# A Newton iteration's squares crossed in all six steps, and one quarter of their copy moved from ScalarE to VectorE

## What is computed

```
K = kernel_2                                  # softmax, 64x64 per image and head
V = 1 / max(sum(K, axis=-2)) * K^T
for _ in range(6):
    KV = K @ V
    V = 0.25 * V @ (13 I - KV @ (15 I - KV @ (7 I - KV)))
```

## Time and profile before

| | |
|---|---|
| median of 3 runs | 690.59 us (689.09 to 691.2) |
| profiled execution, its own time | 694.64 us |
| span in the profile | 692.8 us |
| TensorE matmul busy | 656.4 us (95%) |
| TensorE weight load busy | 574.3 us (83%) |
| VectorE busy | 496.1 us (72%) |
| ScalarE busy | 385.5 us (56%) |
| granted TensorE clock, mean | 0.988 of full |

### The profile page before, as it was taken

How to read it: one execution, slowest core, us unless ns; L and a number is a source line. 1 busy time by engine, 2 the same in 40 slices (tenths; PEclk the granted TensorE clock), 3 DMA queues, 4 the chain that set the end, 5 groups by cost and what they waited for, 6 DMA issues and landing times.

```text
span 692.8 us, 29942 instructions
## 1 busy us (share of the span) xinstructions
PE 656.4 (95%) x13218; PEld 574.3 (83%) x13218; DVE 496.1 (72%) x1351; ACT 385.5 (56%) x1045; POOL 106.5 (15%) x328
## 2 busy tenths in 40 slices
PE   4878999999999999999999998899999999999998
PEld 2667888888888888888888787688999999999997
DVE  5566878888888888888888986576557547556644
ACT  0245776766776776676676766744444444444442
POOL 1212123223212312312312400110000000000000
PEclk9988999999999999999999999999999999999999
DMA  8792121111111111111100000000000000000000
GB/s 310 260 286 82 35 65 34 35 64 35 36 63 35 50 48 35 52 47 35 34 4 5 4 4 4 4 1 2 0 24 1 1 0 24 2 1 23 1 1 23
DMA packets 13425, 30.64 MB, mean 44 GB/s; under 512 B 1264, under 2 KB 7536, under 8 KB 13040
## 3 DMA queue, kind: packets, MB, share of 16 engines
q1 hardware_dynamic: 13296, 28.73, 12.7%
HBM read 27.16 MB, written 1.57 MB: 41 GB/s over the span
## 4 chain that ended last, share of the span: by engine, by line
PE 87%; DVE 6%; ACT 3%; issue 2%; DMA 1%; SPq 1%; POOL 0%; DVEq 0%; POOLq 0%
PE ps L409 29%; PE ps L574 18%; PE ps L564 16%; PE ps L296 6%; PE ps L313 2%; PE ps L374 2%; PE ps L427 2%; PE ps L356 2%; PE ps L314 1%; PE ps L348 1%; DVE uu L857 1%; DVE se L813 1%; DVE sst L811 1%; PE ps L440 1%; PE ps L328 1%
## 5 line engine op out<-in xcount | busy, mean ns | idle before, releaser
L919 DVE SCALAR_TENSOR_TENSOR acc<-ps,comb,acc 128x192 f32<-128x192 f32 x256 | 89.1, 411 | 84.0 <-PE ps L574 83.9
L574 PE MATMUL ps<-w_sb,work 128*128 128x192 f32 x768 | 140.3, 326 | 0.7 <-ACT work L744 0.7
L574 PEld LDWEIGHTS ps<-w_sb,work 128*128 128x128 f32 x768 | 129.3, 189 | 9.0 <-issue 1.1
L744 ACT ACTIVATE work<-ps 128x512 f32<-128x512 f32 x96 | 57.3, 597 | 138.7 <-PE ps L564 138.7
L409 PEld LDWEIGHTS ps<-rr 64*64 64x64 f32 x3840 | 98.2, 135 | 20.3 <-issue 11.9
L409 PE MATMUL ps<-rr 64*64 64x64 f32 x3840 | 110.8, 223 | 4.0 <-issue 3.2
L409 PE MATMUL ps<-uu,qq 64*64 64x64 f32 x4608 | 99.4, 226 | 11.9 <-DVE uu L857 10.3
L857 DVE SCALAR_TENSOR_TENSOR uu<-rr,qq 128x384 f32<-128x384 f32 x160 | 86.5, 563 | 32.5 <-ACT qq L651 24.2
L409 PEld LDWEIGHTS ps<-uu,qq 64*64 64x64 f32 x4608 | 82.9, 135 | 29.5 <-DVE uu L857 19.1
L658 ACT ACTIVATE rr<-ps 128x384 f32<-128x384 f32 x160 | 73.8, 489 | 57.7 <-PE ps L409 57.3
L296 PE MATMUL ps<-weff,xtb 128*128 128x193 f32 x240 | 51.3, 351 | 1.1 <-DVE t L768 1.1
(11 more groups left out here) (142 smaller groups left out, 1070.0 us busy)
## 6 DMA issues: line engine op xcount, KB each, us to landing
xtb<-xt_dram SPq DMA_DIRECT2D x16, 512.0 KB, 3.8
work<-x_dram SPq DMA_DIRECT2D x16, 512.0 KB, 4.1
wsh<-ws_dram SPq DMA_DIRECT2D x10, 288.0 KB, 5.7
w_sb<-w_dram SPq DMA_DIRECT2D x1, 2304.0 KB, 22.3
w_a<-w_dram SPq DMA_DIRECT2D x1, 1536.0 KB, 10.5
w_b<-w_dram SPq DMA_DIRECT2D x2, 768.0 KB, 14.7
out_dram<-acc SPq DMA_DIRECT2D x3, 384.0 KB, 2.6
mult<-copies_dram SPq DMA_DIRECT2D x1, 512.0 KB, 8.2
```

Of the source, the lines that this page charges most:

```text
L574: last = pe.matmul(ps[:, 2 + 2 * (e % 2) + j // 2, (j % 2) * DIM:(j % 2 + 1) * DIM], hid[:, n % 4, j * P:(j + 1) * P], w2_sb[:, c, :], sta ...
L744: act.activation(hid[:, n % 4, :], ps[:, UPB[n % 3], :], ACT.Gelu_apprx_tanh).then_inc(gelu_done, 1)
L919: last = dve.scalar_tensor_tensor(out=a, in0=ps[:, 2 + 2 * (e % 2) + j // 2, (j % 2) * DIM:(j % 2 + 1) * DIM], scalar=comb[:, g * GT + j, ...
```

## The change

`CROSSED` becomes all six steps, and a new table `HALVED` with all six steps is added. In a step of `HALVED`, ScalarE copies image 0 of lane 0 and that half of image 1 which goes to partitions 0 to 63; VectorE copies the half that goes from PSUM partitions 0 to 63 to partitions 64 to 127 of qq. VectorE does this at the head of newton_sum, on the same semaphore (square_done) that ScalarE waits for, and then waits for its own copy (q_half) before uu. ScalarE's second copy raises q_ready by 2, so that the counts stay as they were.

```
-CROSSED = (1, 2, 3, 5)
+CROSSED = (0, 1, 2, 3, 4, 5)
+HALVED = (0, 1, 2, 3, 4, 5)
...
                     q = qq[:, lane].rearrange("p i h n -> p i (h n)")
-                    if lane == 0 and k in CROSSED:
+                    if lane == 0 and k in HALVED:
+                        act.activation(q[:, 0], ps[:, 0, 0:LC], ACT.Copy).then_inc(q_ready, 1)
+                        act.activation(q[0:64, 1], ps[64:128, 1, 0:LC], ACT.Copy).then_inc(q_ready, 2)
+                    elif lane == 0 and k in CROSSED:
                         act.activation(q[:, 0], ps[:, 0, 0:LC], ACT.Copy).then_inc(q_ready, 1)
                         for a in (0, 64):
                             act.activation(q[a:a + 64, 1], ps[64 - a:128 - a, 1, 0:LC], ACT.Copy).then_inc(q_ready, 1)
...
             def newton_sum(k, t, lane):
                 n = 12 * t + 2 * k + lane
                 src = r0 if k == 0 else rr
+                if lane == 0 and k in HALVED:
+                    dve.wait_ge(square_done, n + 1)
+                    dve.tensor_copy(qq[64:128, 0, 1].rearrange("p h n -> p (h n)"), ps[0:64, 1, 0:LC]).then_inc(q_half, 1)
+                    dve.wait_ge(q_half, len(HALVED) * t + HALVED.index(k) + 1)
                 dve.wait_ge(q_ready, 4 * (STEPS * t + k) + 3 + lane)
                 dve.scalar_tensor_tensor(out=uu[:, lane], in0=src[:, lane], scalar=3.0, in1=qq[:, lane],
                                          op0=ALU.mult, op1=ALU.add).then_inc(u_ready, 1)
```

More of the change, by code:

```diff
@@ L159, in vit_block_kernel @@
         y_copied, square_done = sems("y_copied square_done")
-        q_ready, u_ready, prod_done, r_ready, o_done = sems("q_ready u_ready prod_done r_ready o_done")
+        q_half, q_ready, u_ready, prod_done, r_ready, o_done = sems("q_half q_ready u_ready prod_done r_ready o_done")
         o_copied, proj_done, h2_ready = sems("o_copied proj_done h2_ready")
```

## The result

The changed kernel takes **703.97 us** (702.89 to 705.29, four runs) against 690.89 for the kernel before on the same chip: a ratio of 1.0193, 95% interval 1.0175 to 1.021. It is 13.1 us slower, clear of noise. The forecast was 698.0, and the range ended at 702. The sign was right and the size was not.

A forecast was written before the change was run, and what follows sets the result against it. TensorE was taken to bound the kernel (87% of the chain), with VectorE nearly full. Regular tiles 5.4, stopped tiles 0.3, tiles 13 and 14 3.0, tile 15 -1.1, tile 0 -0.2: +7.4 on 690.59 gives 698.0 us; range 691 to 702.

The forecast's parts named there:

- The copy: VectorE's new PSUM copy ahead of lane 0's uu: 0.355 us, costing 0.50 us where VectorE is late.
- Step 1: Newton step 1, where VectorE comes late: uu of both lanes and the products come later, +0.50 us a tile.
- Steps 0, 2 and 5: Newton steps where the copy makes uu or the products slightly later: +0.10, +0.03 and +0.05 us a tile.
- Step 3: Newton step 3, where VectorE idles 0.83 us for ScalarE: lane 0's uu 0.35 us earlier, the step -0.39 us.
- Step 4: Newton step 4, VectorE late again: lane 0's uu late by 0.47 us, 0.25 of it slack; step +0.31 us.
- The sum: All six Newton steps of a regular tile together: +0.60 us a tile, 5.4 us over nine regular tiles.
- tiles 13 and 14: Tiles without token matmuls on TensorE, so steps 2 and 3 also hang on VectorE: +3.0 us together.
- The last tile: Tile 15, where VectorE is idle and the change helps: -1.1 us.
- Step 1 of tiles 3, 8 and 9: TensorE stops 0.6 to 0.7 us inside these squares, covering the copy's price; 0.1 us left each.
- the overlap of the copy with its predecessor: Rival: the copy overlaps its predecessor, costing 0.39 us where VectorE is late; +0.24 a tile, 692.5 us; chance 0.14.
- The saving: Rival: cheap copy, so TensorE's 0.35 and ScalarE's 0.33 us come through; 676 at the ceiling, halfway 685; chance 0.17.
- The copy is longer than its row: Rival: VectorE slowed by 0.13 us at each late place beside others' work; +4.5 on top, 702.5 us; chance 0.12.

The follow-up runs named there:

- the changed kernel with the late add: The changed kernel with GpSimd's residual add moved behind its low_tokens; 702.93 us, ratio 1.0149 to the kernel before.

## Why the prediction was right in sign and wrong in size

- **The copy** was put at 0.355 us from the COPY of L1001; it measured 351 ns (347 to 352), 96 times. The start 0.03 after its predecessor and the 0.035 behind it held too, and the copy that stays at partition 0 showed why. "Where VectorE is the late one, the copy costs 0.50 us": steps 1 and 4 bear it out with 0.51 and, after the slack, 0.37.
- **Step 1**, +0.50: measured +0.509, and +0.506 where it was the only edit.
- **Steps 0, 2 and 5**, +0.10, +0.03, +0.05: measured +0.107, +0.076, +0.018.
- **Step 3**, -0.39: measured -0.009. This is the step that failed, in its first term: "Lane 0's uu is 0.35 earlier". Lane 0's uu started 0.28 us earlier and ended 0.01 earlier, because it ended when the residual add let it, and the products and the rest of the step hung on that end. What the prediction built on the term was sound: with the add moved away, lane 0's uu ended 0.41 earlier, the products started 0.16 earlier (0.18 was said, "held by the Gram matmuls"), and the step took 0.40 less. The clue stood in rows 4, though not plainly: two uu of 1.16 us where steps 1 and 5 have 1.02 and 1.07. Step 4 has 1.16 too, but there each uu takes its 0.55 and lane 1's starts late, while in step 3 lane 0's own uu takes 0.69. The duration of one instruction tells them apart, that of the pair does not. I read it as a general slowness and moved the copy's price by it in a rival, 0.13 at each late place, instead of asking which instruction of another engine overlapped it. GpSimd's row at 190.72 would have put the -0.39 at zero, and the sum at +1.0 a tile.
- **Step 4**, +0.31: measured +0.367. It was reckoned from step 3 starting VectorE 0.43 early and the step 0.39 early, and since neither came, the two errors cancelled but for 0.06. Where both came (the changed kernel with the late add, 0.40 each), step 4 cost 0.44: the 0.04 that the forecast won there was not won, and the last router weight took 0.07 longer beside low_tokens.
- **The sum** of a regular tile was +0.60 and measured +1.07. Over tiles 1 to 12 the prediction had 5.7 us and the two profiled executions differ by 10.4. Step 3's 0.38 in each of twelve tiles is 4.6 of it. With it at zero the forecast would have been 7.4 + 4.6 = 12.0 us, against 13.1 measured; the 1.1 left is about what the small misses of the other five steps come to (0.087 a tile, 1.0). The stops of TensorE differ both ways between the two executions (tile 3 reads +1.9, tile 6 +0.5, tile 9 nothing) and happen to leave little over.
- **The exceptions**: tiles 13 and 14 together +3.0, measured +2.5 (25.95 and 24.83 against 24.00 and 24.28). The last tile -1.1, measured -1.0 from its start to the end of the kernel. Tile 0's -0.2 can't be read, since that tile takes 25.4 to 29.4 us in executions of kernels that hardly differ in it. Step 1 of tiles 3, 8 and 9, at 0.1 each: -0.05, +0.15 and -0.01. That was right, but steps 4 and 5 of tile 3 grew by 1.7 together in this execution.
- **The rivals**: the overlap of the copy with its predecessor is out. The saving did not arrive. "The copy is longer than its row" came nearest with 702.5, for a wrong reason: the copy is not longer (351 ns), nothing is slower at the late places, and uu, not the copy, is what is held.
- **The Trainium skill**: the rule on the held copy was weighed in the prediction and was borne out. The advice to use both ScalarE and VectorE to empty PSUM (TensorEngine Tiling, PSUM Bottleneck) paid in no step of a regular tile. In steps 1 and 4 VectorE was late already, in 0, 2 and 5 the work ahead of uu ended only 0.11, 0.08 and 0.32 us before ScalarE's copies, less than the 0.42 that the new copy takes, and in step 3 the add held uu. It paid in step 3 once the add was out of the way (-0.40), and in the last tile.

## What to carry to other kernels

Moving work from one engine to another pays only where the receiving engine is ready earlier by more than the work costs there, and that is read step by step: the same 0.35 us copy cost 0.5 us where VectorE came late, and the last tile, where VectorE was idle, became shorter by 1.0 us. When the same instruction takes longer at one place than at others (1.16 against 1.02), find the instruction of another engine that overlaps it before pricing any start time there, GpSimd's first where both of its inputs are in SBUF. Tiles in which the same pair lies a little differently are a control that costs nothing (tiles 3 and 9 here). An earlier start wins nothing if the instruction then waits for a neighbour: read ends, not starts.

## What was new about the hardware

- GpSimd's 0.60 us add from SBUF and VectorE's uu from two SBUF operands do not run together: uu ended 0.41 us after the add's end when the add was first (0.69 or 0.95 us instead of 0.56, by how early it started), and the add took 0.97 to 1.02 us when uu was first or started with it. The hold shows as a longer duration, not as idle time.
- A Vector copy of the same size that writes from partition 64 instead of 0 (and reads another PSUM bank) starts 0.03 us after its predecessor's end instead of 0.08 to 0.09 before it.
- Of two semaphore waits ahead of a Vector instruction, the one written last costs 0.07 us more if it ends last (0.10 against 0.03).
- TensorE stops for 0.2 to 1.6 us at a time with nothing that it waits for in the profile, most often at the same places (steps 1 and 4 of tiles 3, 8 and 9) and in varying size: 1.9 to 8.6 us in one execution, in kernels that differ by little. What it is waiting for there stays open. These stops are the largest difference found between executions whose steps are otherwise the same, so a sum of steps is to be trusted to 2 or 3 us here.
